# A float32 expert FFN on one core: where the moving operands of the split products begin in SBUF

## What is computed

```
attn = softmax((x + braak_embed[itok][..., None]) @ side^T) @ side        # per sequence, 256 x 256
nx   = attn * rsqrt(mean(attn^2) + 1e-6) * norm_w
w    = normalized top-2 of softmax(nx @ gate_w^T) over 8 experts
h1   = nx @ w1^T + 2 * (nx @ a1_e^T) @ b1_e^T          # per expert e, rank 16
h3   = nx @ w3^T + 2 * (nx @ a3_e^T) @ b3_e^T
act  = silu(h1) * h3
out  = x + sum_e w_e * (act @ w2^T + 2 * (act @ a2_e^T) @ b2_e^T)
```

## The kernel before

| moving operand | columns | high part | low part |
|---|---|---|---|
| kT0 / kT1 | 256 | 32 / 192 | 96 / 320 |
| probT0 / probT1 | 256 | 64 / 256 | 128 / 448 |
| w2T | 256 | 64 | 160 |
| b2T | 256 | 288 | 416 |
| t, v, br, s | 512 | 0 | 0 |

## Time and profile before

### The profile page before, as it was taken

The page is one execution under the profiler, slowest core; times in us unless marked ns, Lnnn a source line. Parts: engine busy times, 40 slices in busy tenths (PEclk is TensorE's granted clock), DMA queues, the critical chain, the costliest instruction groups (busy, mean ns, idle before and its releaser), DMA issues.

```text
span 1307.0 us, 18607 instructions
## 1 busy us (share of the span) xinstructions
PE 1299.5 (99%) x7286; PEld 1137.2 (87%) x7286; DVE 843.5 (65%) x1558; ACT 526.8 (40%) x991; POOL 249.8 (19%) x213
## 2 busy tenths in 40 slices
PE   8999999999999999999999999999999999999998
PEld 8999998888888888888888888888888888888887
DVE  6776656756665576656675667557675666565556
ACT  6776753333343344333333334333333343243332
POOL 3556540202011020202020202011020202020200
PEclk9999999999999999999999999999999999999999
DMA  9545810020202020201102020202020101102000
GB/s 292 148 147 154 233 44 32 2 73 2 73 2 73 1 73 1 59 16 30 44 2 73 1 73 2 73 1 74 2 73 1 57 17 34 41 1 73 1 17 17
DMA packets 73584, 69.56 MB, mean 53 GB/s; under 512 B 7051, under 2 KB 64793, under 8 KB 73369
## 3 DMA queue, kind: packets, MB, share of 16 engines
q1 hardware_dynamic: 73184, 68.37, 17.7%
q10 hardware_dynamic: 312, 0.02, 0.0%
HBM read 51.27 MB, written 17.10 MB: 52 GB/s over the span
## 4 chain that ended last, share of the span: by engine, by line
PE 98%; ACT 1%; DVE 0%; DMA 0%; SPq 0%; issue 0%; DVEq 0%
PE bank L1204 31%; PE bank L1203 31%; PE bank L1205 30%; PE bank L1329 2%; PE bank L1256 2%; PE bank L1307 1%; PE bank L1249 0%; DMA kv<-in_fside_BxSxS 0%; PE bank L1215 0%; ACT prob L662 0%; SPq L395 0%; ACT kT_hi L646 0%; ACT qT_hi L645 0%; SPq L444 0%; DVE x_out L1147 0%
## 5 line engine op out<-in xcount | busy, mean ns | idle before, releaser
L1075 DVE TENSOR_TENSOR act_a<-silu_a,bank 128x512 f32<-128x512 f32 x128 | 87.7, 685 | 211.0 <-PE bank L1205 194.3
L753 ACT ACTIVATE br_hi<-act_br 128x512 fp32r<-128x512 f32 x128 | 80.9, 632 | 188.6 <-DVE act_br L1086 188.6
L746 ACT ACTIVATE silu_b<-bank 128x512 f32<-128x512 f32 x128 | 76.2, 595 | 187.9 <-PE bank L1205 187.1
L589 POOL TENSOR_TENSOR t_lo<-t_in,t_hi 128x512 fp32r<-128x512 f32 x32 | 40.6, 1289 | 552.2 <-ACT t_hi L733 552.2
L1204 PE MATMUL bank<-w2T_lo,s_hi 128*128 128x256 f32 x512 | 144.7, 283 | 0.0
L1205 PE MATMUL bank<-w2T_hi,s_lo 128*128 128x256 f32 x512 | 143.3, 280 | 0.0
L1203 PE MATMUL bank<-w2T_hi,s_hi 128*128 128x256 f32 x512 | 142.7, 279 | 0.0
L1083 DVE TENSOR_TENSOR act_b<-silu_b,bank 128x512 f32<-128x512 f32 x128 | 88.0, 687 | 81.3 <-PE bank L1205 80.3
L742 ACT ACTIVATE silu_a<-bank 128x512 f32<-128x512 f32 x128 | 75.7, 591 | 134.2 <-PE bank L1205 134.1
L608 POOL TENSOR_TENSOR v_lo<-v_full,v_hi 128x512 fp32r<-128x512 f32 x64 | 94.5, 1508 | 136.7 <-ACT v_hi L738 136.7
L1096 DVE TENSOR_TENSOR br_lo<-act_br,br_hi 128x512 fp32r<-128x512 f32 x128 | 104.8, 819 | 5.6 <-ACT br_hi L753 3.1
(11 more groups left out here) (197 smaller groups left out, 3237.5 us busy)
## 6 DMA issues: line engine op xcount, KB each, us to landing
kv<-in_fside_BxSxS SPq DMA_DIRECT2D x32, 256.0 KB, 3.1
x_in<-in_x SPq DMA_DIRECT2D x32, 256.0 KB, 3.9
t_scratch<-oT SPq DMA_DIRECT2D x32, 256.0 KB, 2.5
t_in<-t_scratch SPq DMA_DIRECT2D x16, 512.0 KB
x_out<-in_x SPq DMA_DIRECT2D x16, 512.0 KB, 3.9
out<-x_out SPq DMA_DIRECT2D x30, 256.0 KB, 4.0
rho<-scale_scratch SPq DMA_DIRECT2D x16, 256.0 KB
rstd<-scale_scratch SPq DMA_DIRECT2D x16, 256.0 KB
```

The lines of the kernel that those rows point to most:

```text
L746: nc.scalar.activation(silu_b[:, :], h1_bank[j % 2][:, :], ACT.Silu).then_inc(silu_b_ready, 1)
L753: nc.scalar.activation(br_hi[j % 2][:, :], act_br[j % 2][:, :], ACT.Copy).then_inc(br_hi_ready, 1)
L1075: nc.vector.tensor_tensor(act_a[j % 2][:, :], silu_a[j % 2][:, :], h3_bank[j % 2][:, :], ALU.mult).then_inc(act_a_ready, 1)
```

## The change

Gaps and padding are changed, nothing else: no instruction is added, removed or moved, and each engine's instructions stand in the same order as before. All moving operands of the short products (kT, probT, w2T, b2T) now begin 64 bytes past a multiple of 512 in their high part and 320 bytes past one in their low part. The same is done to t, v and br, which are moving operands of long products. s keeps its place at 0 and 0: it moves in three of the long products of a chunk (`down_z`) and is stationary in `down_y`. So 3648 of the 4032 long matmuls change (384 move s). The stationary operands stay on multiples of 512; the padding behind each group brings the tensors after it back there.

```diff
-        w2T = split("w2T", [P, FC, D], gaps=(16, 24))
-        a2T = split("a2T", [P, FC, ER], gaps=(88, 0))
+        w2T = split("w2T", [P, FC, D], gaps=(16, 64))
+        a2T = split("a2T", [P, FC, ER], gaps=(48, 0))
...
-        b2T = split("b2T", [ER, D], gaps=(72, 32))
-        sb(ctx, "pad_b2T", [P, 24])
+        b2T = split("b2T", [ER, D], gaps=(16, 64))
+        sb(ctx, "pad_b2T", [P, 48])
...
-        kT = [split(f"kT{k}", [P, DC * S], early, ((8, 16), (24, 32))[k]) for k in range(2)]
+        kT = [split(f"kT{k}", [P, DC * S], early, ((16, 64), (64, 64))[k]) for k in range(2)]
...
-        probT = [split(f"probT{k}", [P, SC * S], early, ((16, 16), (32, 48))[k]) for k in range(2)]
-        sb(early, "pad_probT", [P, 16])
+        probT = [split(f"probT{k}", [P, SC * S], early, ((16, 64), (64, 64))[k]) for k in range(2)]
+        sb(early, "pad_probT", [P, 48])
...
+        sb(late, "pad_t_hi", [P, 16])
         t_hi = [sb(late, f"t_hi{k}", [P, DC, TILE], F32R) for k in range(2)]
+        sb(late, "pad_t_lo", [P, 64])
         t_lo = [sb(late, f"t_lo{k}", [P, DC, TILE], F32R) for k in range(2)]
+        sb(late, "pad_mask", [P, 48])
...
+        sb(late, "pad_v_hi", [P, 16])
         v_hi = [sb(late, f"v_hi{k}", [ER, TILE], F32R) for k in range(4)]
+        sb(late, "pad_v_lo", [P, 64])
         v_lo = [sb(late, f"v_lo{k}", [ER, TILE], F32R) for k in range(4)]
+        sb(late, "pad_silu", [P, 48])
...
         s_hi = [sb(late, f"s_hi{k}", [P, TILE], F32R) for k in range(S_RING)]
         s_lo = [sb(late, f"s_lo{k}", [P, TILE], F32R) for k in range(S_RING)]
+        sb(late, "pad_br_hi", [P, 16])
         br_hi = [sb(late, f"br_hi{k}", [P, TILE], F32R) for k in range(2)]
+        sb(late, "pad_br_lo", [P, 64])
         br_lo = [sb(late, f"br_lo{k}", [P, TILE], F32R) for k in range(2)]
+        sb(late, "pad_z", [P, 48])
```

## The result

The changed kernel takes 1326.41 us (median of 4 runs, 1326.24 to 1326.52) against 1308.99 us for the kernel before on the same chip: a ratio of 1.0134, with a 95% interval of 1.0122 to 1.0146. The prediction was 1300.8 us with a range of 1283 to 1314. The time lies outside the range and on the other side. Of the prediction's cases the nearest is rival B, slower by a mean step of some 232 ns, which had a chance of 0.16.

The account below looks back on a forecast made before the run. PE's steps from matmul start to matmul start were taken to bound the kernel; 8.4 us saved on long products and nothing counted elsewhere took 1309.2 to 1300.8 us, range 1283 to 1314.

Parts of the forecast that it names:

- rival B: Long products: starts jumping 256 bytes from pass to pass make every shifted one pay 232.9 ns, 1332 us; chance 0.16.
- What bounds the kernel: Whole kernel: PE's steps from one matmul's start to the next set the time; PE has no waits.
- That the start addresses of the moving operands matter, against the stationary ones: Split products on PE: moving reads and next weights' reads interfere, start addresses setting how often; 11 to 13 ns aren't columns.
- The term of the long products: 3648 long products of t, v, br: overhead falls from 13.3 to 11.0 ns, saving 8.4 us.
- s at 0/0 among shifted ones: Three products with s per chunk: possible short settling at each alignment change, 1 to 2 us lost, not counted.
- Short products: Some 2500 products with kT, probT, w2T, b2T: no gain taken, 1.5 us either way kept for the range.
- Settling: Long products behind short ones: seven at 6.2 ns over, four places a tile, about 2 us in all; not counted.
- Other engines: DVE, ACT and POOL: buffers move by 64 or 320 bytes, no effect on time since PE waits for nobody.

Follow-up runs that it names:

- the chains: Kernels leaving out the whole computation, PE alone issuing runs of matmuls from chosen operand starts; settled long step 226.7 ns at 0/0, 229.0 at 64/320.
- the pinned chains: Chains of 48 matmuls on PE alone with stationary, moving or both operands one repeated SBUF word; long step 231.0 to 231.7 ns stationary pinned, 216.7 moving pinned.
- first chain kernel: Whole computation left out, PE alone issuing chains of 48 matmuls at various starts, lengths and widths; long 226.7 ns at 0/0, short 113.3 at 192/192.

## Why the prediction was wrong

*What bounds the kernel: right.* PE's steps set the time and nothing else moved. Two sentences went too far. The list of waits does have rows of PE, and the row that the earlier trace rows calls its last is not the last; and some of PE's groups do have idle time ahead of them. They are five waits of 0.5 to 1.0 us, 3.5 us in all, of which this is the longest; four of the five stand in the changed kernel too.

```profile
PE bank L1215 <- DVE gram_diag L832: 1.0, 1, 1.0
```

*That the start addresses of the moving operands matter, against the stationary ones: right,* by the chains. That two reads of PE cross is still a theory: the pinned chains fit it in part and do not prove it.

*The term of the long products: wrong, and the cause of the miss.* The prediction had no long product with another start and took the overhead of the short ones, 11.0 ns, because they "read the same kinds of operands with the same weight loads but begin off 512". The length of the product counts as much as the start. In the chains 0/0 costs 13.3 ns over the columns at either length, but 64/320 costs 11.1 at 256 columns and 15.6 at 512. 192/192 is the best place for short products (6.7) and among the worst for long ones: by the first chain kernel 20.0. So the term of -8.4 us was in truth +6.9 us for the place alone, s included. I called the neighbours of another length the nearest rows. The rows of long products themselves, and the earlier trace rows, show the same addresses at 226.7 and at 232.9 ns, so that the settled step is one that can be lost.

*s at 0/0 among shifted ones: the direction right, the size wrong.* I put "1 to 2 us lost" on it and did not count it. It cost 10.5 us, more than the place itself. I had priced only a short settling at each change of alignment. The trace after shows products that keep a slower rhythm until the next short run.

*Rival B: the right sign and nearly the right size, at 0.16, and half the right reason.* Its mean step was 232.9, the measured one 231.7. That is in part luck: the measured mean is made of products at 229 ns and others at 233, of two causes, where B had one. For it stood, where long products that follow others at a different place run at 228 to 239 ns. Against it I held that short products jump from pass to pass and have less overhead, the same step across lengths that failed above. That the long products lose a rhythm which rests on high, low and s beginning alike is what the run with s moved bears out. That jumps of 256 bytes disturb them is wrong: 64/64 and 64/320 cost the same.

*Short products: right.* No change within 1 us was forecast, and there is none. *Settling:* about 2 us in the kernel was right too; in the kernels with other short places it vanishes, and 1.9 to 2.2 us are gained.

*Other engines: right*, no effect.

*The Trainium skill.* "PE and ACT never wait on anyone" ("SBUF — State Buffer", "Who interferes with whom") would have given no change. As to other engines the runs agree: a chain of PE alone at 0/0 takes the same 226.7 ns as the kernel. As to no change they contradict it: with PE alone at work a long split product takes 226.7 ns at 0/0, 233.3 when the stationary operands alone move to 64, and 226.7 again when the moving ones follow, so PE's two operands are not free of each other. The 2.5 ns over the columns of "TensorE: Matmul & The Clock Gate", "Back-to-back issue gap", agrees with the bf16 chain (215.7 - 213.3 = 2.4) and not with float32r.

## What to carry to other kernels

When PE is bound by its own steps and not by waits, divide a long run of equal products by their number and compare it with their columns; what is over can depend on where moving and stationary operands begin against each other. Do not carry such an overhead from one length or neighbourhood to another: measure it for each length, in the order in which the kernel issues its products, since a chain by itself gave 113.3 ns where the kernel gave 117.9. And move all operands of one kind together or none: here the three products in a chunk that were left at the old place cost more (10.5 us) than the new place itself (6.9 us).

## What the runs showed of the hardware that I had not expected

- The pattern repeats when either start moves by 256 bytes, and steps of less than 32 bytes count as well: 226.7 ns at 0, 236.7 at 4 bytes, 231.7 at 16, 228.9 at 12.
- The same products at the same addresses can run in different rhythms, 229.0 or 233.3 ns, for 24 products and more, depending on what ran ahead of them.
- Fewer stationary columns do not reduce the overhead at 0/0: 13.3 ns at 128, 16.7 at 96 and at 64, 18.3 at 32. This is unexplained.
- At 0/0, 128 and 192 columns both take 111.7 ns a step, so under 256 columns something else than the columns sets the step of a float32r product; 320 and 384 columns are again 13.3 over theirs, 448 are 16.
- A bf16 product of 512 columns pays 2.4 ns and a float32r product with its moving operand pinned to one word 3.3; the full price appeared only in chains whose moving operand is four bytes wide and walks. (In the bf16 chain the stationary operand is two bytes wide as well, so the two are not told apart.)
